# A four-block graph and expert network on one core: X ahead of weights, results ahead of weights, another start of the relational pipeline, and its later roots on ScalarE and VectorE

## The chip, the core and the metric

One core of one Trainium2 chip runs the whole program as one launch. The time is that of the device, in microseconds (us), for one execution. The kernel before was run three times: 1425.54, 1429.92 and 1430.27 us, median 1429.92. One further execution was profiled.

## What is computed

The input is 128 graphs of 64 nodes with 128 features each (8192 rows) and an adjacency matrix of 64 x 64 integers (0 or 1 in these inputs) for each graph. Four blocks follow one another, each with a residual:

```
x = x + gated_graph(layernorm(x), adj)      # 3 layers of a GRU cell on A^T (h W_l), A = (adj != 0)
x = x + experts_1(layernorm(x))             # top 2 of 8, softmax of the two scores, 128 -> 512 relu -> 128
x = x + relational(layernorm(x), adj)       # below
x = x + experts_2(layernorm(x))             # top 2 of 8, each with its layernorm gains, 128 -> 512 gelu -> 128

def _direction(x, W, Wg, b, bg, adj, rel_ids):
    h = x @ W.T
    g = h @ Wg.T
    vals = (h[:, :, None, :] + b) * sigmoid(g[:, :, None, :] + bg)
    onehot = (adj[..., None] == rel_ids).astype(h.dtype)
    return einsum('bnmr,bmrd->bnd', onehot, vals)
relational = relu(_direction(.., "fwd", adj, 2..40) + _direction(.., "bwd", adj^T, 2..40) + _direction(.., "loop", adj^T, [1]))

def _layernorm(x, axis=-1, eps=1e-05):
    m = jnp.mean(x, axis=axis, keepdims=True)
    v = jnp.var(x, axis=axis, keepdims=True)
    return (x - m) / jnp.sqrt(v + eps)
```

Relations 2 to 40 do not occur in these inputs. Their code stands behind a branch on a flag (`general`), on every engine, and is not entered.

## The kernel before, in words

**Tiles and stages.** X stays in SBUF as 64 tiles of 128 rows (two graphs each); 4 tiles are a group (GT), 16 groups the whole. Products run in float16 as a high and a low part. The stages: `opening` (loads, first norm, weights cut into parts), `gated_graph`, `experts "1"`, `relational`, `experts "2"`, `combine`. `hand_over` is a barrier of four engines between a graph stage and its experts; `phase` ends in a barrier of all. Experts work on rows that POOL scattered to their slots (`send`, L643: one indirect DMA for one tile and one of its two choices), and write to `results` in DRAM. The next stage fetches these (`fetch`, L1677, two DMAs a group) and adds them to X (`mix`, L1667, whose two adds appear as L1673).

**The opening's queues.** ScalarE's queue issues X in four loads, then ADJ (L423, L424); behind them stand ScalarE's own instructions, first the cast of the norm (L386). SP's queue issues 20-odd small loads (L286) and then the expert weights W1 and W2 of 2 MB each (L308, L310).

**The gated graph's queue.** SP stores 16 pieces of the second experts' weights to `kept` as they are cut (`keep`, L867), fetching the next ones between (`bring`, L863), and transposes rows by DMA (`turn_start`, L882; `turn`, L874). Groups are worked in quads; `turn_start(QUAD)` transposes the four tiles of the first group of the second quad, for TensorE's first product of it.

**The relational pipeline.** `relational` is written out as 21 steps s = 0 to 20 (`steps`). Each engine runs its own `step(s)` in a fixed order, and in a step works on several groups:

- VectorE: `mixture(s)` (results added, moments, var_a), `los_a(s-1)`, `los_c(s-4)`, `sums(s-3)` (residual add at L2045, moments, var_c at L2050), `values(s-2)`, `scores(s-4)` (L2109, L2113), `router`, `shifts_a(s)` (L2022, c_shift_a), `shifts_c(s-3)`, `v_los(s-2)`.
- ScalarE: `turned_a(s-1)`, `turned_b(s-4)` (c_xT_a, c_xT_b, out of PSUM), `v_his(s-2)`, `norms_a(s)`, `norms_c(s-3)` (each four norms and a cast; the latter's into ROWS), `weigh` (prob, by Sigmoid), `sig(s-1)` (c_sg), `relu(s-2)` (c_rl).
- TensorE: `turn_a(s-1)`, `turn_b(s-4)`, `scores(s-4)`, `values(s-1)`, `neighbours(s-2)`, `rank`.
- POOL: `roots(s)`, one pow (L1793) of both variances to the power −0.5 into c_rs, then SENDS[s] sends.

`router` chooses experts for a batch of two groups (`first_choice`, `second_choice`, L580 to L599) in the step in which the later group has its scores, and in the step after gives them places (`place`, L629 to L637, writes pos). So batches are chosen at s = 5, 7, 9, ... and placed at 6, 8, 10, ...; sends begin at s = 6 with eight a step, four a step from s = 16, 96 in all; the other 32 follow in the experts' stage. After the sixth batch VectorE also makes the table of blocks (`early_table`). SP first reloads the experts' weights from `kept` (2 x 2 MB, L1808), then packs the relations' rows (L1810), then fetches groups 0 and 1, and each later group when a buffer is free.

Of the kernel before, what the change touches and what calls it, by code (L numbers as in the profile page):

```python
# [16 lines left out]
F32 = mybir.dt.float32  # L17
# [225 lines left out]
def opening(nc, block, keep, over, ins, k):  # L243
# [6 lines left out]
    with ExitStack() as ctx:  # L250
# [33 lines left out]
        def _(sp):  # L284
# [22 lines left out]
            small(gbf[:, 1, :], ins["L1_ffn_br"].rearrange("(a e) -> a e", a=1).to_broadcast([P, E]))  # L307
            sp.dma_start(stage[0][:, :].rearrange("p (n d) -> p n d", d=P),  # L308
# [463 lines left out]
def gated_graph(nc, block, keep, over, ins, k, sent):  # L772
# [14 lines left out]
    with ExitStack() as ctx:  # L787
# [70 lines left out]
        def _(sp):  # L858
# [28 lines left out]
            for i in four:  # L887
                bring(i)
            for i in range(N_PIECE):
# [6 lines left out]
            turn_start(QUAD)  # L896
# [786 lines left out]
BATCH = 2  # L1683
ROUTED = 4
EARLY_BATCH = 5


def relational_sends(NG):

    first = ROUTED + BATCH - 1 + 1  # L1690
    n = NG + ROUTED + 1
    wanted = [0 if s < first else 4 * BATCH if s < NG else CARRY for s in range(n)]
# [4 lines left out]
def batch_at(s, late):  # L1697

    n = s - late - ROUTED - BATCH + 1
    return (n // BATCH, late) if n >= 0 and n % BATCH == 0 and n // BATCH < 16 // BATCH else (None, None)  # L1700


def relational(nc, block, keep, over, ins, k, sent):
# [6 lines left out]
    with ExitStack() as ctx:  # L1710
# [38 lines left out]
        gathered = [sem(f"fetched{p}") for p in two]  # L1749
        half, full = sem("half"), sem("full")  # L1750
# [30 lines left out]
        def _(pool):  # L1781
# [4 lines left out]
            def roots(s):  # L1786
                lo, hi = 0 if s < NG else GT, 3 * GT if 3 <= s < NG + 3 else GT
                if s < NG:
                    pool.wait_ge(var_a, s + 1)
                if 3 <= s < NG + 3:  # L1790
                    pool.wait_ge(var_c, s - 2)
                if lo < hi:
                    pool.tensor_tensor(rstd[s % 4][:, lo:hi], var[s % 2][:, lo:hi], k["mhalf"][:, lo:hi], ALU.pow)\  # L1793
                        .then_inc(rooted, 1)

            def step(s):
                roots(s)
                n = sum(SENDS[0:s])
                for i in range(n, n + SENDS[s]):
                    if i % (2 * T) == 0:  # L1800
                        pool.wait_ge(Q.placed, i // (2 * T) + 1)
                    send(pool, k, k["slots"][1], sent, i)
# [415 lines left out]
```

## Time and profile before

| what | us |
|---|---|
| runs, median (range) | 1429.92 (1425.54 to 1430.27) |
| the profiled execution: its own time, its span | 1423.04, 1420.9 |
| opening | 0 to 87.6 |
| gated graph | to about 480 |
| experts 1 | to 800.5 |
| relational | to 1057.4 |
| experts 2, combine | to 1420.9 |
| busy in the span: TensorE, VectorE, ScalarE, POOL | 912.6, 904.0, 763.7, 732.9 |

The span is from the first to the last instruction of the profiled execution; its own time contains a little more. Ends of stages are read from the barriers between them. A busy share of an engine is a mean over stages with different limits, so the list of instructions of a stage, with the idle time before each and what released it, tells more than the table.

### The profile page before, as it was taken

To read this page: it belongs to the slowest core of one execution; us is meant where nothing else is said; L and a number is where in the kernel's file an instruction comes from. 1 tells how busy PE (TensorE), PEld (TensorE's weight loads), DVE (VectorE), ACT (ScalarE), POOL (GpSimd) and SP (SyncE) were. 2 spreads that over 40 slices of the span, in tenths; PEclk is the share of its full clock that TensorE was granted. 3 is DMA by queue.
4 is the path that set the end of the run, shared out by engine and by line. 5 is a ranking of instruction groups with operands and counts; after the bars stand their busy time and mean duration, and the time that the engine had idled before them with its cause. 6 is when DMAs were issued, how large, how long until landed. Compare 5 with 4: busy or idle time off the path is not lost. (4 is left out here: it accounts for less than half of the span.)

```text
span 1420.9 us, 23073 instructions
## 1 busy us (share of the span) xinstructions
PE 912.6 (64%) x5849; PEld 517.1 (36%) x5850; DVE 904.0 (64%) x2437; ACT 763.7 (54%) x1390; POOL 732.9 (52%) x714
## 2 busy tenths in 40 slices
PE   1367778878873267789887066655522877878830
PEld 1244434444432123334576033333311433346620
DVE  5968789999986426556555167776653655544536
ACT  2477757777752135557566056555531765655720
POOL 3511123767757646556555314777666456554550
PEclk9999999999985569999899555555556999988975
DMA  9233221221201514333322421221122353232209
GB/s 266 75 113 95 83 47 28 56 63 46 61 20 39 137 44 107 84 82 70 69 57 53 163 75 61 66 86 49 40 50 65 81 118 75 65 77 59 54 25 349
DMA packets 198299, 115.61 MB, mean 81 GB/s; under 512 B 154988, under 2 KB 175614, under 8 KB 197408
## 3 DMA queue, kind: packets, MB, share of 16 engines
q1 hardware_dynamic: 168144, 69.54, 20.5%
q0 software_dynamic: 17408, 34.13, 7.5%
q10 hardware_dynamic: 12624, 10.49, 2.6%
q8 instruction: 54, 0.88, 0.3%
q14 instruction: 69, 0.57, 0.1%
HBM read 43.80 MB, written 51.61 MB: 67 GB/s over the span
## 5 line engine op out<-in xcount | busy, mean ns | idle before, releaser
L643 POOL DMA_INDIRECT slots<-ROWS,pos x256 | 265.2, 1036 | 90.4 <-issue 71.1
L1510 POOL DMA_INDIRECT results<-e1ys,e1home x144 | 155.8, 1082 | 126.7 <-DVE e1ys L1638 85.8
L1510 POOL DMA_INDIRECT results<-e2ys,e2home x144 | 152.2, 1057 | 131.2 <-DVE e2ys L1638 91.3
L1585 ACT ACTIVATE e1hf<-psum,VT 128x512 f32<-128x512 f32 (+1 forms) x192 | 104.4, 583 | 141.6 <-PE psum L207 82.4
L1604 DVE SCALAR_TENSOR_TENSOR e1hs<-e1hf,e1hs 128x512 f16<-128x512 f32 x144 | 95.9, 691 | 119.4 <-ACT e1hs L1591 77.9
L1585 ACT ACTIVATE e2hf<-psum,VT 128x512 f32<-128x512 f32 (+1 forms) x192 | 104.2, 582 | 123.0 <-remote 69.9
L1604 DVE SCALAR_TENSOR_TENSOR e2hs<-e2hf,e2hs 128x512 f16<-128x512 f32 x144 | 95.1, 689 | 105.5 <-ACT e2hs L1591 81.7
L1362 POOL TENSOR_TENSOR a_Z<-a_Z,a_H 128x512 f32<-128x512 f32 x48 | 68.2, 1422 | 163.2 <-ACT a_Z L1092 160.5
L205 PE MATMUL psum<-e1xT,W 128*128 128x512 f16 (+1 forms) x192 | 67.5, 352 | 43.9 <-issue 22.3
L205 PE MATMUL psum<-a_hT,WHH 128*128 128x512 f16 x144 | 59.4, 412 | 55.6 <-ACT a_Z L1092 47.4
L205 PE MATMUL psum<-e2hs,W 128*128 128x512 f16 (+1 forms) x192 | 64.9, 338 | 42.7 <-DVE e2hs L1604 36.6
L1591 ACT ACTIVATE e2hs<-e2hf 128x512 f16<-128x512 f32 x144 | 86.9, 633 | 0.0
L1591 ACT ACTIVATE e1hs<-e1hf 128x512 f16<-128x512 f32 x144 | 86.9, 631 | 0.0
L205 PE MATMUL psum<-e1hs,W 128*128 128x512 f16 (+1 forms) x192 | 67.0, 349 | 29.5 <-DVE e1hs L1604 21.5
L205 PE MATMUL psum<-e2xT,W 128*128 128x512 f16 (+1 forms) x192 | 66.0, 344 | 28.7 <-ACT e2hf L1585 11.8
L1793 POOL TENSOR_TENSOR c_rs<-c_var,mhalf 128x12 f32<-128x12 f32 (+2 forms) x19 | 38.2, 2012 | 75.1 <-DVE c_var L2050 52.4
L1938 ACT ACTIVATE c_norm_a<-X,c_shift_a,c_rs 128x128 f32<-128x128 f32 x64 | 26.3, 482 | 80.3 <-DVE c_shift_a L2022 72.1
L206 PE MATMUL psum<-e1xT,W 128*128 128x512 f16 (+1 forms) x192 | 67.7, 353 | 2.1 <-issue 2.1
L207 PE MATMUL psum<-e2xT,W 128*128 128x512 f16 (+1 forms) x192 | 65.4, 341 | 5.1 <-issue 5.1
L207 PE MATMUL psum<-e1xT,W 128*128 128x512 f16 (+1 forms) x192 | 67.5, 351 | 1.4 <-issue 1.4
L206 PE MATMUL psum<-e1hs,W 128*128 128x512 f16 (+1 forms) x192 | 66.8, 348 | 2.1 <-issue 2.1
L206 PE MATMUL psum<-e2xT,W 128*128 128x512 f16 (+1 forms) x192 | 65.8, 343 | 2.7 <-issue 2.7
(363 smaller groups left out, 2676.9 us busy)
## 6 DMA issues: line engine op xcount, KB each, us to landing
c_G<-results SPq DMA_DIRECT2D x32, 256.0 KB
d_G<-results SPq DMA_DIRECT2D x32, 256.0 KB, 5.0
slots<-slots SPq DMA_DIRECT2D x16, 264.0 KB
W<-in_L_ffn_W_dram SPq DMA_DIRECT2D x16, 256.0 KB, 3.4
kept<-a_cut SPq DMA_DIRECT2D x16, 256.0 KB, 2.6
slots<-ROWS,pos POOLq DMA_INDIRECT x256
W<-kept SPq DMA_DIRECT2D x2, 2048.0 KB, 10.1
out_dram<-X ACTq DMA_DIRECT2D x16, 256.0 KB, 7.2
```

The source lines that it names most:

```text
L205: pe.matmul(out, lhs(0), rhs(0), start=start, stop=False, skip_group_check=True)
L206: pe.matmul(out, lhs(0), rhs(1), start=False, stop=False, skip_group_check=True)
L207: return pe.matmul(out, lhs(1), rhs(0), start=False, stop=stop, skip_group_check=True)
L643: pool.indirect_dma_start(out=slots, out_offset=bass.IndirectOffsetOnAxis(ap=k["pos"][:, c, t:t + 1], axis=0), in_=k["ROWS32"][:, t, :], i ...
L1362: pool.tensor_tensor(Z[p % 2][:, :], Z[p % 2][:, :], H[p][:, :], ALU.mult).then_inc(zh_sb, 1)
L1510: pool.indirect_dma_start(out=k["results"][m], out_offset=bass.IndirectOffsetOnAxis(ap=home[:, GT * b + q:GT * b + q + 1], axis=0), in_=ys ...
L1585: t = act.activation(hf[c][:, cols], HB[c][:, cols], func, bias=VT[:, bass.ds(e * CH + b1_col + c, 1)], scale=1 / PS)
L1591: act.activation(hs[j][:, 0, c, :], hf[c][:, :], ACT.Copy, scale=AS).then_inc(h_hi, 1)
L1604: dve.scalar_tensor_tensor(out=hs[j][:, 1, c, :], in0=hf[c][:, :], scalar=AS, in1=hs[j][:, 0, c, :], op0=ALU.mult, op1=ALU.subtract).then_ ...
L1793: pool.tensor_tensor(rstd[s % 4][:, lo:hi], var[s % 2][:, lo:hi], k["mhalf"][:, lo:hi], ALU.pow)\
L1938: i = act.activation(out[:, q, :], tile_of(X, GT * g + q), ACT.Identity, bias=shift[:, q:q + 1], scale=scale[:, q:q + 1])
```

## The change

Four edits.

1. In `opening` SP waits for the last load of X (`x_in[LOADS - 1]`) before it issues W1 and W2.
2. In `gated_graph` SP's `turn_start(QUAD)` moves from behind the loop over the 16 pieces to ahead of it.
3. In `relational` SP fetches groups 0 and 1 first, then packs the rows. The weights come back in eight parts of 512 KB, one each behind the fetch of g = 2 to 9.
4. In `relational` the batches are group 0 alone, group 1 alone, and then pairs; they are chosen at s = 4, 5, 7, 9, ... and sends begin at s = 5 with 8, 6 and 2, then eight a step. `place` (`put`) stands between `los_a` and `los_c`. In steps 0 to 5 (`SPLIT`) `shifts_a` and `norms_a` stand early in the step, POOL takes the two roots apart, with up to two sends between, and the choice stands at the step's end. From step 6 on POOL takes no root: ScalarE takes the square root (`deviations`, 13 calls) and VectorE inverts it and makes one step of Newton's on it (`inverses`, four operations, each waiting for the one before).

```diff
@@ opening, SP
+            sp.wait_ge(x_in[LOADS - 1], 16)
             sp.dma_start(stage[0][:, :].rearrange("p (n d) -> p n d", d=P),
...
@@ gated_graph, SP
             for i in four:
                 bring(i)
+            turn_start(QUAD)
             for i in range(N_PIECE):
...
-            turn_start(QUAD)
...
-BATCH = 2
+BATCHES = [(0, 1), (1, 1)] + [(g, 2) for g in range(2, 16, 2)]
 ROUTED = 4
-EARLY_BATCH = 5
+SPLIT = 6
...
-    wanted = [0 if s < first else 4 * BATCH if s < NG else CARRY for s in range(n)]
+    wanted = [0 if s < first else (8, 6, 2)[s - first] if s < first + 3 else 8 if s < NG else CARRY for s in range(n)]
...
@@ relational, POOL
+            def step(s):
+                n, m = sum(SENDS[0:s]), sum(SENDS[0:s + 1])
+                if 3 <= s < SPLIT:
                     pool.wait_ge(var_a, s + 1)
+                    root_of(s, 0, GT)
+                    ahead = min(n + 2, m)
+                    sends(n, ahead)
                     pool.wait_ge(var_c, s - 2)
+                    root_of(s, GT, 3 * GT)
+                    sends(ahead, m)
+                else:
+                    if s < 3:
+                        pool.wait_ge(var_a, s + 1)
+                        root_of(s, 0, GT)
+                    sends(n, m)
...
@@ relational, SP
-            for n, w in enumerate((k["W1"], k["W2"])):
-                sp.dma_start(w[:, :, :].rearrange("p s n -> p (s n)"), k["kept"][n]).then_inc(back, 16)
+            for g in two:
+                fetch(sp, k, 0, g, G[g], gathered[g])
...
+                if 2 <= g < 10:
+                    weights(g - 2)
...
@@ relational, ScalarE
+            def deviations(s):
+                lo, hi = columns_at(s, NG)
+                if s < NG:
+                    act.wait_ge(var_a, s + 1)
+                if s < NG + 3:
+                    act.wait_ge(var_c, s - 2)
+                    act.activation(deviation[s % 2][:, lo:hi], var[s % 2][:, lo:hi], ACT.Sqrt).then_inc(spread, 1)
...
                     turned_a(s - 1, (s - 1) % 2)
+                if s < SPLIT:
+                    norms_a(s, s % 2)
...
                     v_his(s - 2, s % 2)
-                if s < NG:
+                if s >= SPLIT:
+                    deviations(s)
+                if SPLIT <= s < NG:
                     norms_a(s, s % 2)
...
@@ relational, VectorE
+            def inverses(s):
...
+                dve.wait_ge(spread, n + 1)
+                dve.reciprocal(y, deviation[p][:, lo:hi]).then_inc(newton, 1)
+                dve.wait_ge(newton, 4 * n + 1)
+                dve.scalar_tensor_tensor(out=t, in0=y, scalar=-0.5, in1=v, op0=ALU.mult, op1=ALU.mult).then_inc(newton, 1)
+                dve.wait_ge(newton, 4 * n + 2)
+                dve.tensor_tensor(t, t, y, ALU.mult).then_inc(newton, 1)
+                dve.wait_ge(newton, 4 * n + 3)
+                dve.scalar_tensor_tensor(out=rstd[s % 4][:, lo:hi], in0=t, scalar=1.5, in1=y, op0=ALU.add, op1=ALU.mult)\
+                    .then_inc(newton, 1)
+                dve.wait_ge(newton, 4 * n + 4)
...
                     los_a(s - 1, (s - 1) % 2)
+                put(s)
+                if s < SPLIT:
+                    shifts_a(s, s % 2)
...
                     scores(s - 4)
-                router(s)
-                if s < NG:
+                if s >= SPLIT:
+                    choose(s)
+                    inverses(s)
+                if SPLIT <= s < NG:
                     shifts_a(s, s % 2)
...
                     v_los(s - 2, s % 2)
+                if s < SPLIT:
+                    choose(s)
...
```

The order of the built programs at three places follows. Names ahead of the arrow are written, those behind it read. L numbers of the changed program are its own. Semaphores keep the name of the first that had their number, so n_... there is one of the relational stage.

SP at the start of the relational stage, before:

```order
L1808 DMA W<-kept 128x8192 x2
L1810 DMA relrows<-in_L_gnn_b_fwd_dram 39x128
L1810 DMA relrows<-in_L_gnn_bg_fwd_dram 39x128
L1810 DMA relrows<-in_L_gnn_b_bwd_dram 39x128
L1810 DMA relrows<-in_L_gnn_bg_bwd_dram 39x128
L1680 DMA c_G<-results 128x512 x4
L1680 DMA c_G<-results 128x512 [waits c_full,n_x_in2]
L1680 DMA c_G<-results 128x512
```

and now:

```order
L1681 DMA c_G<-results 128x512 x4
L1841 DMA relrows<-in_L_gnn_b_fwd_dram 39x128
L1841 DMA relrows<-in_L_gnn_bg_fwd_dram 39x128
L1841 DMA relrows<-in_L_gnn_b_bwd_dram 39x128
L1841 DMA relrows<-in_L_gnn_bg_bwd_dram 39x128
L1681 DMA c_G<-results 128x512 [waits c_full,n_x_in0]
L1681 DMA c_G<-results 128x512
```

The two loads of W stood ahead of all; now the four DMAs of groups 0 and 1 do.

ScalarE in a step with a choice of experts, before:

```order
L1976 ACTIVATE c_xT_b<-psum 128x1024 [waits n_chain,n_small_sb]
L1959 ACTIVATE c_vs<-c_sg 128x512 [waits n_empty_set,n_w_in1]
L1938 ACTIVATE c_norm_a<-X,c_shift_a,c_rs 128x128 [waits c_shifted_a]
L1938 ACTIVATE c_norm_a<-X,c_shift_a,c_rs 128x128 x3
L1946 ACTIVATE c_tok_a<-c_norm_a 128x512 [waits c_norm_as]
L1938 ACTIVATE c_norm_c<-X,c_shift_c,c_rs 128x128 [waits c_shifted_c]
L1938 ACTIVATE c_norm_c<-X,c_shift_c,c_rs 128x128 x3
L1953 ACTIVATE ROWS<-c_norm_c 128x4x128 [waits c_norm_cs]
L604 ACTIVATE prob<-v_gap 128x8 [waits v_gapped]
L605 ACTIVATE ROWS<-v_gap 128x8
```

and now (the square root first writes c_deviation):

```order
L2015 ACTIVATE c_xT_b<-psum 128x1024 [waits n_consts,n_chain]
L1990 ACTIVATE c_vs<-c_sg 128x512 [waits n_small_done,n_empty_out]
L1998 ACT_TABLE_LOAD [waits c_var_c]
L1998 ACTIVATE c_deviation<-c_var 128x12 [waits c_var_a]
L1969 ACTIVATE c_norm_a<-X,c_shift_a,c_rs 128x128 [waits c_shifted_a]
L1969 ACTIVATE c_norm_a<-X,c_shift_a,c_rs 128x128 x3
L1977 ACTIVATE c_tok_a<-c_norm_a 128x512 [waits c_norm_as]
L1969 ACTIVATE c_norm_c<-X,c_shift_c,c_rs 128x128 [waits c_shifted_c]
L1969 ACTIVATE c_norm_c<-X,c_shift_c,c_rs 128x128 x3
L1984 ACTIVATE ROWS<-c_norm_c 128x4x128 [waits c_norm_cs]
L605 ACT_TABLE_LOAD
L605 ACTIVATE prob<-v_gap 128x8 [waits v_gapped]
```

A load of a table now stands in front of the square root, behind c_vs, and another in front of prob; in a step without a choice the second stands in front of c_sg. There are 13 of each.

VectorE in a step that places a batch, from the scores to c_shift_a, before:

```order
L2109 TENSOR_TENSOR S<-psum,c_rs 128x32 [waits n_chain]
L2113 TENSOR_TENSOR S<-S,gate_b 128x32 [waits n_consts]
L629 TENSOR_TENSOR v_wide<-psum,base 128x64 [waits v_ranked]
L630 TENSOR_TENSOR base<-psum,base 128x8 [waits v_chain]
L631 TENSOR_TENSOR v_wide<-v_wide 128x128 [waits v_chain]
L634 TENSOR_TENSOR ROWS<-prob,ROWS 128x8 [waits v_weighed,v_chain]
L636 TENSOR_REDUCE v_row<-v_wide 128x16
L637 CAST pos<-v_row 128x2x8 [waits v_chain]
L2022 SCALAR_TENSOR_TENSOR c_shift_a<-c_mv,c_rs 128x4 [waits c_rooted]
```

Now the place stands in the first half of such a step, between the two subtractions L240:

```order
L240 SCALAR_TENSOR_TENSOR c_tok_a<-c_norm_a,c_tok_a 128x512 [waits n_w_sb]
L630 TENSOR_TENSOR v_wide<-psum,base 128x64 [waits v_ranked]
L631 TENSOR_TENSOR base<-psum,base 128x8 [waits v_chain]
L632 TENSOR_TENSOR v_wide<-v_wide 128x128 [waits v_chain]
L635 TENSOR_TENSOR ROWS<-prob,ROWS 128x8 [waits v_weighed,v_chain]
L637 TENSOR_REDUCE v_row<-v_wide 128x16
L638 CAST pos<-v_row 128x2x8 [waits v_chain]
L240 SCALAR_TENSOR_TENSOR ROWS<-c_norm_c,ROWS 128x4x128 [waits n_lo]
L2108 TENSOR_TENSOR X<-X,c_rl 128x512 [waits n_small_sb]
```

and from the scores to c_shift_a there are these:

```order
L2172 TENSOR_TENSOR S<-psum,c_rs 128x32 [waits n_consts]
L2176 TENSOR_TENSOR S<-S,gate_b 128x32 [waits n_small_in]
L2071 RECIPROCAL c_guess<-c_deviation 128x12 [waits c_spread]
L2073 SCALAR_TENSOR_TENSOR c_slope<-c_guess,c_var 128x12 [waits c_newton]
L2075 TENSOR_TENSOR c_slope<-c_slope,c_guess 128x12 [waits c_newton]
L2077 SCALAR_TENSOR_TENSOR c_rs<-c_slope,c_guess 128x12 [waits c_newton]
L2084 SCALAR_TENSOR_TENSOR c_shift_a<-c_mv,c_rs 128x4 [waits c_newton]
```

The six operations of the place have left the stretch ahead of c_shift_a, and four of the inverse have come in.

## Rows read from the trace of the kernel before

**Rows 1.** Busy time by stage: window, length, busy us (instructions) by engine, PEclk, DMA share, GB/s.
```profile
0.00:87.60 87.60, 24.72 (x156) 19.24 (x157) 68.14 (x294) 39.03 (x60) 32.51 (x48) 1.00 0.51 138
...
800.50:814.90 14.40, 0.00 (x0) 0.00 (x0) 0.93 (x1) 0.00 (x0) 1.25 (x39) 0.50 0.92 367
...
877.00:1010.00 133.00, 80.98 (x562) 43.89 (x560) 92.62 (x427) 73.62 (x153) 99.59 (x83) 0.50 0.21 67
```

**Rows 2.** Relational stage before the sends, VectorE: start us, us, engine, line, operation, idle before.
```profile
854.05 0.16 DVE L2022 SCALAR_TENSOR_TENSOR c_shift_a<-c_mv,c_rs 128x4 f32<-128x4 f32 x1 [1.47 <-POOL c_rs L1793]
...
859.84 0.69 DVE L2045 TENSOR_TENSOR X<-X,c_rl 128x512 f32<-128x512 f32 x1 [0.35 <-ACT c_rl L1928]
...
866.20 0.15 DVE L2022 SCALAR_TENSOR_TENSOR c_shift_a<-c_mv,c_rs 128x4 f32<-128x4 f32 x1
...
876.89 0.16 DVE L2022 SCALAR_TENSOR_TENSOR c_shift_a<-c_mv,c_rs 128x4 f32<-128x4 f32 x1 [0.19 <-POOL c_rs L1793]
```

**Rows 3.** Relational stage with sends, VectorE.
```profile
940.94 0.69 DVE L2045 TENSOR_TENSOR X<-X,c_rl 128x512 f32<-128x512 f32 x1 [0.21 <-issue]
...
947.06 0.19 DVE L2109 TENSOR_TENSOR S<-psum,c_rs 128x32 f32<-128x32 f32 x1 [3.17 <-remote]
...
950.56 0.15 DVE L2022 SCALAR_TENSOR_TENSOR c_shift_a<-c_mv,c_rs 128x4 f32<-128x4 f32 x1
...
1009.46 0.15 DVE L2022 SCALAR_TENSOR_TENSOR c_shift_a<-c_mv,c_rs 128x4 f32<-128x4 f32 x1
```

**Rows 4.** Waits from 877 to 1010 (us in total, times, longest), and POOL's root there.
```profile
DVE S L2109 <- PE psum L207: 20.0, 6, 4.5
...
DVE c_shift_a L2022 <- POOL c_rs L1793: 0.4, 2, 0.2
...
L1793 POOL TENSOR_TENSOR c_rs<-c_var,mhalf 128x12 f32<-128x12 f32 x9 | 20.7, 2303 | 4.4 <-DVE c_var L2050 4.2
```

**Rows 5.** One step with sends, TensorE and ScalarE.
```profile
944.08 0.17 PE L207 MATMUL psum<-WGATE,c_xT_b 128*128 128x8 f16 x1
...
939.25 0.63 ACT L1953 ACTIVATE ROWS<-c_norm_c 128x512 f16<-128x512 f32 x1
939.78 0.64 ACT L1933 ACTIVATE c_sg<-psum 128x256 f32<-128x256 f32 x2
...
950.75 1.65 ACT L1938 ACTIVATE c_norm_a<-X,c_shift_a,c_rs 128x128 f32<-128x128 f32 x4 [6.20 <-DVE c_shift_a L2022]
```

**Rows 6.** Opening, the same lists, of SP, ScalarE and VectorE.
```profile
11.68 0.90 SPq L308 DMA_DIRECT2D n_stage<-in_L_ffn_W_dram  x1
...
14.63 5.69 ACTq L424 DMA_DIRECT2D ADJ<-in_adj_dram  x1
...
22.31 0.69 DVE L240 SCALAR_TENSOR_TENSOR ROWS<-n_norm,ROWS 128x512 f16<-128x512 f32 x1 [8.46 <-ACT ROWS L386]
```

**Rows 7.** Gated graph, the same lists, of SP and TensorE.
```profile
94.84 1.76 SPq L863 DMA_DIRECT2D W<-in_L_ffn_W_dram  x4
...
102.55 0.60 SPq L867 DMA_DIRECT2D kept<-a_cut  x1
...
179.17 6.47 SPq L882 DMA_TRANSPOSE a_hT<-ROWS  x5
...
185.55 0.58 PE L205 MATMUL psum<-a_hT,WHH 128*128 128x512 f16 x1 [2.91 <-DMA a_hT<-ROWS]
```

**Rows 8.** Hand-over, SP and VectorE, and the page's DMA issue (KB each, us to landing).
```profile
805.29 1.99 SPq L1680 DMA_DIRECT2D c_G<-results  x4
...
814.95 1.42 DVE L1673 TENSOR_TENSOR X<-X,c_G 128x512 f32<-128x512 f32 x2 [13.45 <-DMA c_G<-results]
...
d_G<-results SPq DMA_DIRECT2D x32, 256.0 KB, 5.0
```

**Rows 9.** The table load of the last experts, ScalarE.
```profile
1063.61 1.28 ACT L1585 ACT_TABLE_LOAD   x1 [10.40 <-PE psum L207]
1064.91 1.26 ACT L1585 ACTIVATE e2hf<-psum,VT 128x512 f32<-128x512 f32 x2
```

More of the change, by code:

```diff
@@ L1680, in fetch, with chosen_at, rooted_by, columns_at @@
         sp.dma_start(G[:, c, :, :], rows[:, c, bass.ds(GT * g, GT), :]).then_inc(sem, 16)
-BATCH = 2
+BATCHES = [(0, 1), (1, 1)] + [(g, 2) for g in range(2, 16, 2)]
 ROUTED = 4
-EARLY_BATCH = 5
+SPLIT = 6
 def relational_sends(NG):
-    first = ROUTED + BATCH - 1 + 1
+    first = ROUTED + 1
     n = NG + ROUTED + 1
-    wanted = [0 if s < first else 4 * BATCH if s < NG else CARRY for s in range(n)]
+    wanted = [0 if s < first else (8, 6, 2)[s - first] if s < first + 3 else 8 if s < NG else CARRY for s in range(n)]
     early = 2 * GT * (NG - QUAD)
     return [max(min(w, early - sum(wanted[0:s])), 0) for s, w in enumerate(wanted)]
-def batch_at(s, late):
-    n = s - late - ROUTED - BATCH + 1
-    return (n // BATCH, late) if n >= 0 and n % BATCH == 0 and n // BATCH < 16 // BATCH else (None, None)
+def chosen_at(s):
+    for b, (g, n) in enumerate(BATCHES):
+        if g + n - 1 + ROUTED == s:
+            return b, g, n
+    return None, None, None
+def rooted_by(s):
+    return sum(1 if n < 3 else 2 for n in range(min(s + 1, SPLIT)))
+def columns_at(s, NG):
+    return (0 if s < NG else GT), (3 * GT if s < NG + 3 else GT)
 def relational(nc, block, keep, over, ins, k, sent):
@@ L1784, in _, with root_of, sends @@
             i.then_inc(rv_set, 1)
-            def roots(s):
-                lo, hi = 0 if s < NG else GT, 3 * GT if 3 <= s < NG + 3 else GT
-                if s < NG:
+            def root_of(s, lo, hi):
+                pool.tensor_tensor(rstd[s % 4][:, lo:hi], var[s % 2][:, lo:hi], k["mhalf"][:, lo:hi], ALU.pow)\
+                    .then_inc(rooted, 1)
+            def sends(n, m):
+                for i in range(n, m):
+                    for b, (g, groups) in enumerate(BATCHES):
+                        if i == 2 * GT * g:
+                            pool.wait_ge(Q.placed, b + 1)
+                    send(pool, k, k["slots"][1], sent, i)
+            def step(s):
+                n, m = sum(SENDS[0:s]), sum(SENDS[0:s + 1])
+                if 3 <= s < SPLIT:
                     pool.wait_ge(var_a, s + 1)
-                if 3 <= s < NG + 3:
+                    root_of(s, 0, GT)
+                    ahead = min(n + 2, m)
+                    sends(n, ahead)
                     pool.wait_ge(var_c, s - 2)
[L1792 to L1802, printed above, removed]
+                    root_of(s, GT, 3 * GT)
[5 more added lines that the diff above has]
+                    sends(n, m)
             steps(pool, step)
@@ L1806, in _, with weights @@
         def _(sp):
-            for n, w in enumerate((k["W1"], k["W2"])):
-                sp.dma_start(w[:, :, :].rearrange("p s n -> p (s n)"), k["kept"][n]).then_inc(back, 16)
+            def weights(i):
+                n, part = i // 4, slice(i % 4 * E * HID // 2, (i % 4 + 1) * E * HID // 2)
+                w = (k["W1"], k["W2"])[n]
+                sp.dma_start(w[:, :, :].rearrange("p s n -> p (s n)")[:, part], k["kept"][n][:, part]).then_inc(back, 16)
+            for g in two:
+                fetch(sp, k, 0, g, G[g], gathered[g])
             for n, name in enumerate(("b_fwd", "bg_fwd", "b_bwd", "bg_bwd")):
                 sp.dma_start(relrows[:, n * P:(n + 1) * P], ins["L1_gnn_" + name]).then_inc(rows_packed, 16)
-            for g in two:
-                fetch(sp, k, 0, g, G[g], gathered[g])
             sp.wait_ge(rows_packed, 64)
```

53 lines of the change are left out of this document (32 added, 21 removed).

## The prediction

> **What bounds the kernel now.** I read the table of stages first [rows 1]. The stages follow one another, most of them with a barrier between, so an edit in one is worth what it moves that stage's end, and nothing later hides it. The change touches four: the opening (0 to 87.6 us, VectorE busy 68.1), the gated graph (to 480), the gap from 800.5 to 814.9, in which no engine computes while the DMA share is 0.92, and the relational stage (to 1057.4). No engine fills the last: in 133 us of it POOL is busy 99.6, VectorE 92.6, TensorE 81.0 and ScalarE 73.6. So a chain through the engines bounds it, at a granted clock of 0.50 (1.2 GHz) throughout.
>
> What that chain is the rows of VectorE show, if a step is read as two halves. The first runs from c_shift_a (L2022) to the residual add (L2045): 5.79 us at 854.05, norms, casts and relu on ScalarE back to back. The second runs to the next c_shift_a: 6.36 us with a choice of experts (859.84 to 866.20); the step after, without one, lasts 10.69 in all [rows 2]. There POOL sends nothing, and a pair of steps takes 22.84. Once it sends, a second half with a choice takes 9.62 (940.94 to 950.56), and the nine steps from 876.89 to 1009.46 take 14.73 each, 29.5 a pair [rows 2, 3]: 3.3 us more a step. POOL's root is not the cause, VectorE waits for it 0.4 us in 133 [rows 4]. TensorE's signals arrive late: at 947.06 VectorE starts on scores, 3.17 us idle, whose last matmul began at 944.08 [rows 3, 5]; waits for TensorE in front of the scores sum to 20.0 us in 6 times [rows 4]. Why they are late no row says. This decides the case: the root that the change takes from POOL is not what the chain waits for.
>
> **Opening.** The expert weights (2 x 2 MB) go behind X. ScalarE's queue issues X and then ADJ; ADJ's issue takes 5.69 us, to 20.32, behind it stands the first cast, and VectorE idles 8.46 us for that [rows 6]. From 11.68, when SP issues the weights, to 20.32 two queues share the DMA engines. Alone, ScalarE's would need about half of these 8.6 us: the gain is between 0 and 4.3, I take **−3.3**, nearer the upper end since the wait of 8.46 is larger than all of it. VectorE's 68.1 busy us lie almost all behind that wait, so the gain carries through. The weights come no later in sum: the same bytes, at a DMA share of 0.51 over the stage [rows 1].
>
> **Gated graph.** The four transposes of quad 1 move on SP ahead of the 16 pieces. Five such issues take 6.47 us, four 5.2; SP is free from 96.60 to the first store of a piece at 102.55 [rows 7]. They fit, and the pieces stay where they are. TensorE's 2.91 us at 185.55 for a_hT go [rows 7]: 0 to −2.9. I take **−2.9**; what is late next there would be ScalarE's own chain.
>
> **Hand-over.** SP issues 4 MB of weights and four row loads, then at 805.29 the results, and VectorE starts at 814.95 [rows 8]. The same fetch in the last stage lands after 5.0 us (median) [rows 8]. Issued at 800.5, it starts VectorE at about 806: **−8.9**, the bounds −9.6 (every us of the wait but 4.8) and −4 (only the issues' 4.8 saved, less 0.8). The weights come back in eight parts at steps 2 to 9 beside a DMA share of 0.21 [rows 1], and are needed by the experts alone: nothing.
>
> **Steps 4 to 6.** Groups 0 and 1 are now chosen one by one: one choice and one place more. The choice, 13 chained operations, is 3.05 of the 3.50 us from 947.06 to 950.56 [rows 3], 0.23 us each; the place, six of that kind, 1.4; for four tiles instead of eight both a little less, 4.1 together. Step 6's own loads and Newton are 2.2 (below): 6.3 us. The sends start one step earlier, and with them TensorE's late signals: up to 3.3 more. Between +6.3 and +9.6 I take **+7**, near the lower end, because step 7 now sends only two. Most of the head start is spent here.
>
> **Steps 7 to 15.** From step 6 ScalarE's table is switched twice a step, to Sqrt's and back to Sigmoid's: 13 x 2 = 26 loads by 1.28 us [rows 9]. The first waits for c_var_c and runs where ScalarE waits for c_shift_a anyway, 6.20 us at 950.75 [rows 5]: free where TensorE's signal is late. The second stands between the cast into ROWS and c_sg (or prob), and behind it c_rl, on which L2045 waits. ScalarE has no gap there, 939.25 + 0.63 overlaps 939.78 [rows 5]: **+1.28** a step. On VectorE reciprocal and Newton are four chained operations by 0.23, put between the scores (or the choice) and c_shift_a: **+0.9** a step, in place of a root that cost 0. The place, 1.4 in every second step, moves to where VectorE waits for ScalarE: −0.7 a step at best. A step grows by 1.5 (place hidden whole) to 2.5 (nothing hidden, and the first load in series after c_var_c against one pow of 2.30 [rows 4]). I take 1.9, a little under the middle since the late signals do cover the first load: 9 x 1.9 = **+17**. POOL's 20.7 us of pow in 133 [rows 4] are saved on an engine that this chain does not wait for.
>
> The Trainium skill ("ScalarE: Activation LUTs", section on table sets as the hidden batching unit) wants calls of one set kept together and switches few; this change makes 26. The same page adds a drain of about 1.38 us to each switch. The trace disagrees at the one switch that I show: the Gelu starts 0.02 us after its load ends [rows 9]. By the page this term would be larger by an estimated 26 x 1.38 = 36 us.
>
> **Tail.** Steps 16 to 18 keep loads and Newton but have no norms_a that waits for them. Between 0 and 3 x 2.5 = 7.5; I take **+3**. The last place opens the experts, whose own stages do not change.
>
> **Sum.** −3.3 −2.9 −8.9 +7 +17 +3 = +11.9. The profiled execution took 1423.04 us (span 1420.9), so one like it 1434.9. The median of the runs shown, 1429.92, lies 6.9 above: **1442** as a median, slower by 0.8%.
>
> **Rivals.**
> A: TensorE's late signals come from POOL being nearly full. For it: they are late only where POOL sends. Against it: it still sends as much, and only the 20.7 of its 99.6 busy us go [rows 1, 4]. If two thirds of the 3.3 us a step go in ten steps, that is −22 on my sum: **1420**. It is ahead of no change from 12 us on, 1.2 a step. Faster, 0.17.
> B: the lateness is a time that passes anyway, and part of the added work runs inside it; the 3.17 us at 947.06 are room [rows 3]. ScalarE's rows without a gap behind c_shift_a are against [rows 5]. Then a step grows by 0.6 to 1.2, and the sum is 0 to +6: 1430 to 1436. Within 0.5%, 0.25.
> C: a switch between two calls that lie close together costs ScalarE more than the load, because it must first run empty; taken as the load's own length once more, 26 x 1.28 = +33 on mine: 1475. Against it is the start right behind the load [rows 9], though that one followed an idle of 10.40 us. Slower, 0.04. The Trainium skill's drain ("ScalarE: Activation LUTs", what a table load costs) would be this rival.
> D: the gap does not close, because the results' own short packets fill the DMA engines, not the weights. For it: the share is still 0.92 up to 814.9; against it the 5.0 us of the last stage [rows 1, 8]. +5 on mine, the other end of that term: 1447. Slower, 0.06.
>
> **How the numbers follow.** Half a per cent, 7.1 us, is about what a measurement of this kernel can tell from no change: 1422.8 and 1437.1. Faster 0.17 (A); same 0.25 (B); slower 0.58 (C, D and my own case with 0.48). My own case alone, by the bounds of its terms: 1438 to 1455. To leave out no more than 2 in 10, the range takes in B and half of A: **1419 to 1457**; C and the better half of A stay out.
>
> **What would show it.** 26 more table loads of 1.28 us, the next operation right behind each. VectorE's first add of results near 806. ADJ's issue over by about 17. No wait for a_hT. From c_shift_a to L2045 7.0 us instead of 5.8, steps of 16 to 17 us instead of 14.7, TensorE's signals still late, POOL idle longer. Wrong if steps last 14.7 or less (A; B if up to 15.9), if what follows a load starts over 1 us after its end (C), or if VectorE still starts at 811 or later (D). If the second halves shrink by more than the place's 1.4, A is at work.

## The result, and the profile after

The changed kernel took 1479.47 us as a median of 4 runs (1474.44 to 1485.31), the kernel before 1430.1 (4 runs, 1425.54 to 1451.79). The ratio is 1.0364, 95% interval 1.0298 to 1.043: slower by 49 us, where 12 were forecast. The time lies above the range, which ended at 1457. The profiled execution has a span of 1483.5 us against 1420.9. Here and below a median is of all runs, while a ratio leaves out runs more than 1.5% above the fastest of their kernel, so the two can differ by some tenths of a per cent (after_3 and paced_2 below were profiled in such a longer run).

Where the 62.6 us of the spans are, read from the first and last instructions of each stage:

| stretch | before | after | forecast for it |
|---|---|---|---|
| to the start of the gated graph | 88.1 | 86.1 | −3.3 |
| gated graph, to the first product of experts 1 | 392.2 | 391.8 | −2.9 |
| experts 1, to VectorE's first instruction of the relational stage | 320.3 | 328.0 | 0 |
| from there to the first add of results | 14.4 | 4.4 | −8.9 |
| from there to the first product of experts 2 | 247.1 | 302.8 | +27 |
| experts 2 and the last fetch | 358.9 | 370.4 | 0 |

The expert stages' code is the same. Over the profiled executions on chips where the kernel before takes over 1400 us, experts 1 lasts 317 to 348 us whatever the kernel, so the 19 us that the two expert rows grow tell nothing. What tells is the fifth line: +55.7.

First the small edits. ScalarE's, VectorE's and SP's rows of the opening, after, which answer to [rows 6]:

```profile
14.57 3.88 ACTq L425 DMA_DIRECT2D ADJ<-in_adj_dram  x1
...
20.43 0.69 DVE L240 SCALAR_TENSOR_TENSOR ROWS<-n_norm,ROWS 128x512 f16<-128x512 f32 x1 [6.98 <-ACT ROWS L387]
...
22.42 0.90 SPq L309 DMA_DIRECT2D n_stage<-in_L_ffn_W_dram  x1
```

ADJ's issue takes 3.88 us instead of 5.69 and ends at 18.45, not 17. VectorE's first subtraction moves from 22.31 to 20.43: −1.9. (SP's issue of the weights has moved from 11.68 to 22.42.) At the hand-over (SP, then VectorE, as in [rows 8]):

```profile
805.81 2.04 SPq L1681 DMA_DIRECT2D c_G<-results  x4
...
810.28 1.42 DVE L1674 TENSOR_TENSOR X<-X,c_G 128x512 f32<-128x512 f32 x2 [3.49 <-DMA c_G<-results]
```

SP issues the results within 0.1 us of the barrier and VectorE adds them 4.4 us after it: −10.0, a little more than the −8.9 forecast.

Now the relational stage, the table of stages (window, length, busy us by engine, PEclk, DMA share, GB/s; compare [rows 1]):

```profile
0.00:85.70 85.70, 23.71 (x156) 18.42 (x158) 68.12 (x294) 39.03 (x60) 32.51 (x48) 0.72 0.53 141
...
875.00:1047.50 172.50, 84.68 (x585) 44.71 (x584) 101.41 (x479) 102.97 (x183) 70.67 (x72) 0.50 0.20 61
```

The numbers behind the length are TensorE's products, its weight loads, VectorE, ScalarE and POOL. VectorE is busy 101.4 of 172.5 us and POOL 70.7, both a smaller share than before; the granted clock is 0.50, as it was, so the clock does not explain the growth. (In the opening it reads 0.72 where it was 1.00, but VectorE, busy 68.12 us as before, carries that stage, and it ends 1.9 us earlier.) So the engines stand still somewhere. VectorE's rows of two steps (compare [rows 3]):

```profile
894.88 0.16 DVE L2084 SCALAR_TENSOR_TENSOR c_shift_a<-c_mv,c_rs 128x4 f32<-128x4 f32 x1
...
902.57 0.69 DVE L2108 TENSOR_TENSOR X<-X,c_rl 128x512 f32<-128x512 f32 x1
...
908.61 0.16 DVE L2084 SCALAR_TENSOR_TENSOR c_shift_a<-c_mv,c_rs 128x4 f32<-128x4 f32 x1
...
925.89 0.69 DVE L2108 TENSOR_TENSOR X<-X,c_rl 128x512 f32<-128x512 f32 x1 [11.68 <-ACT c_rl L1959]
...
933.12 0.16 DVE L2084 SCALAR_TENSOR_TENSOR c_shift_a<-c_mv,c_rs 128x4 f32<-128x4 f32 x1
```

From one c_shift_a to the next is a step. The one from 908.61, at whose end experts are chosen, takes 24.5 us, the one from 894.88, in which places are given, 13.7: 38.2 a pair, against 29.5 before and 33 forecast. The first half of the long one, 5.8 us before and 7.0 forecast, is 17.3, of which VectorE waits 11.68 for c_rl. POOL in the same time, and the two waits summed over 875 to 1047.5:

```profile
902.17 1.15 POOL L644 DMA_INDIRECT slots<-ROWS,pos  x1 [17.66 <-DVE pos L638]
...
921.66 0.96 POOL L644 DMA_INDIRECT slots<-ROWS,pos  x1 [0.30 <-issue]
940.41 1.15 POOL L644 DMA_INDIRECT slots<-ROWS,pos  x1 [17.79 <-DVE pos L638]
```

```profile
POOL slots L644 <- DVE pos L638: 73.9, 5, 17.8
...
DVE X L2108 <- ACT c_rl L1959: 48.4, 5, 11.7
```

POOL sends sixteen times in one run, 902.17 to 922.6, then waits 17.79 us for the next positions. Before, a root stood between each eight:

```profile
946.63 2.30 POOL L1793 TENSOR_TENSOR c_rs<-c_var,mhalf 128x12 f32<-128x12 f32 x1
949.13 1.03 POOL L643 DMA_INDIRECT slots<-ROWS,pos  x1 [0.20 <-issue]
```

That root starts right behind the eighth send, which ends at 946.61, and the late signal of [rows 3, 5] is there at 947.06. ScalarE and TensorE in the changed kernel's run of sixteen:

```profile
906.20 1.28 ACT L1998 ACT_TABLE_LOAD   x1
907.49 0.21 ACT L1998 ACTIVATE c_deviation<-c_var 128x12 f32<-128x12 f32 x1
...
913.33 1.28 ACT L1964 ACT_TABLE_LOAD   x1
914.62 0.38 ACT L1964 ACTIVATE c_sg<-psum 128x256 f32<-128x256 f32 x1
922.35 0.38 ACT L1964 ACTIVATE c_sg<-psum 128x256 f32<-128x256 f32 x1 [7.34 <-DMA n_stage<-in_L_ffn_W_dram]
925.26 0.60 ACT L1959 ACTIVATE c_rl<-psum 128x512 f32<-128x512 f32 x1 [2.53 <-remote]
```

```profile
910.11 0.42 PE L207 MATMUL psum<-WREL,c_xT_a 128*128 128x256 f16 x1
...
911.17 0.21 PE L1895 MATMUL psum<-WGATE,ident 128*128 128x8 f16 x1
...
927.75 0.19 PE L205 MATMUL psum<-WGATE,c_xT_b 128*128 128x8 f16 x1 [12.19 <-ACT c_xT_b L2015]
```

TensorE's last product of the values is at 910.11, and the small product that closes the neighbours at 911.17. In the code c_sg waits for TensorE alone (the DMA that its row names as releaser belongs to the opening), and c_rl for TensorE and an earlier add of VectorE's; "remote" names no releaser. ScalarE, which waits for both products in turn, gets the first at 922.35, as the last send ends (922.6), and the second at 925.26, 2.6 us behind it. TensorE itself then stands 12.19 us, since c_xT_b could not be made. This is the kind of late signal that stood there before (3.17 us of idle, [rows 3, 5]), grown with the length of POOL's run.

Not every signal is late. The scores' last product is at 905.01, 2.8 us into the run, and VectorE starts on them at 905.74. The values' first half, with its last product at 907.53, is used at 914.62, inside the run. Between VectorE and ScalarE nothing is late at all: c_shift_a starts at 908.61, and the first norm behind it at 908.80. Nor do all late ones wait for the very end: over the four long steps of this trace the values' last product is used 8.6 to 14.4 us after its start, between 3.9 us before the run's end and 1.8 after it, the neighbours' 14.0 to 14.2 us after theirs, 2.6 behind the run's end. "Held for the run" below is short for this.

And nothing drains at a table load: 906.20 + 1.28 is followed by the square root at 907.49, 913.33 + 1.28 by c_sg at 914.62. The further 1.38 us that the Trainium skill states ("ScalarE: Activation LUTs", what a table load costs) is at none of these loads.

### The profile page after: what moved, and what is told of

It reads as the page before. It is cut to its first block and busy times, and to the rows that moved or that the text cites. A ratio compares the mean times of both kernels' runs of the same rounds, so it can differ in the third digit from the quotient of the medians.

```text
span 1483.5 us, 23181 instructions
## 1 busy us (share of the span) xinstructions
PE 924.2 (62%) x5850; PEld 518.3 (35%) x5851; DVE 916.2 (62%) x2508; ACT 803.0 (54%) x1431; POOL 701.3 (47%) x704
## 5 line engine op out<-in xcount | busy, mean ns | idle before, releaser
L644 POOL DMA_INDIRECT slots<-ROWS,pos x256 | 260.3, 1017 | 201.7 <-DVE pos L638 92.1
L205 PE MATMUL psum<-e2hs,W 128*128 128x512 f16 (+1 forms) x192 | 66.7, 347 | 59.8 <-DVE e2hs L1605 53.3
L205 PE MATMUL psum<-e1hs,W 128*128 128x512 f16 (+1 forms) x192 | 66.7, 347 | 29.4 <-DVE e1hs L1605 19.4
L207 PE MATMUL psum<-e1hs,W 128*128 128x512 f16 (+1 forms) x192 | 66.1, 344 | 3.7 <-issue 3.7
L206 PE MATMUL psum<-e1hs,W 128*128 128x512 f16 (+1 forms) x192 | 66.5, 346 | 2.6 <-issue 2.6
L207 PE MATMUL psum<-e2hs,W 128*128 128x512 f16 (+1 forms) x192 | 66.4, 346 | 1.2 <-issue 1.1
```

Source lines behind the costliest of these rows:

```text
L205: pe.matmul(out, lhs(0), rhs(0), start=start, stop=False, skip_group_check=True)
L206: pe.matmul(out, lhs(0), rhs(1), start=False, stop=False, skip_group_check=True)
L207: return pe.matmul(out, lhs(1), rhs(0), start=False, stop=stop, skip_group_check=True)
L644: pool.indirect_dma_start(out=slots, out_offset=bass.IndirectOffsetOnAxis(ap=k["pos"][:, c, t:t + 1], axis=0), in_=k["ROWS32"][:, t, :], i ...
```

## The experiments

Two theories. **Theory 1**: taking the roots from POOL took away what tied POOL to the steps; its sends go out in runs of sixteen, and TensorE's signals are held for such a run. **Theory 2**: the 26 table loads and their surroundings on ScalarE cost it.

The runs fell on chips of two kinds, and this became part of the finding. On one kind the kernel before takes 1404 to 1452 us (called H below, since signals are held there), on the other 1235 to 1245 (called N). Kernels that were measured together ran on one chip, and all ratios are against before on the same chip. The first expectations of paced, no_load, pool_roots and queues were written when only H was known, so that their times in us are times of H; those four ran on N. "Stage" is the time from the first add of results to the first product of experts 2 in the profiled execution.

| kernel | kind | median | ratio (95%) | stage |
|---|---|---|---|---|
| before | H | 1430.1 | 1 | 247.1 |
| the change | H | 1479.5 | 1.036 (1.030 to 1.043) | 302.8 |
| after_again, the same | H | 1466.7 | 1.036 (1.026 to 1.047) | 300.5 |
| after_3, the same | H | 1487.4 | 1.041 (1.025 to 1.057) | 302.0 |
| after_4, the same | N | 1246.3 | 1.006 (1.004 to 1.008) | 253.1 |
| paced_2 | H | 1435.1 | 1.007 (1.001 to 1.013) | 261.2 |
| paced | N | 1244.4 | 1.005 (1.003 to 1.006) | 253.2 |
| pauses | H | 1418.7 | 1.002 (0.997 to 1.007) | 254.0 |
| no_load_3 | H | 1475.8 | 1.035 (1.023 to 1.048) | 292.2 |
| no_load, no_load_2 | N | 1222.4, 1224.1 | 0.987, 0.988 | 230.9, 231.3 |
| pool_roots_3 | H | 1436.9 | 1.007 (0.992 to 1.022) | 249.1 |
| pool_roots, pool_roots_2 | N | 1227.6, 1227.4 | 0.992, 0.991 | 235.8, 236.2 |
| queues_3 | H | 1427.9 | 0.992 (0.972 to 1.012) | 246.6 |
| queues, queues_2 | N | 1221.7, 1222.2 | 0.986, 0.986 | 230.0, 230.0 |
| queues_split | N | 1243.5 | 1.004 (1.002 to 1.005) | 252.2 |
| queues_pause | N | 1232.8 | 0.995 (0.992 to 0.997) | 240.4 |
| no_sends | H | 1541.2 | 1.087 (1.075 to 1.098) | (374.9) |

**The change itself, again.** `after_again` and `after_3` fell on H, `after_4` on N.

> The changed kernel itself, beside the kernel before on the same chip. In the runs of the first comparison TensorE's signals were held while POOL sent (23 and 28 late signals); in the four runs that followed, on another chip (before: 1238 us), none was late. Theory 1 (the loss is held signals times bursts): where the chip holds no signal the change is worth about 1.0047 like the paced form, 1.000 to 1.008; where it holds them, 1.03 or more. Theory 2 (the loss is in the loads): 1.03 or more on either.

> The changed kernel itself beside before, on whichever chip. Theory 1 (runs of 16 sends times held signals): 1.03 to 1.04 where before takes over 1400 us, 1.003 to 1.008 where it takes 1238. Theory 2 (26 table loads alone): the same loss in us on both, 40 to 50.

> The changed kernel itself beside before. Where before takes 1238 us no signal is held and theory 1 expects 1.003 to 1.008, since POOL's runs of 16 sends then hold nothing up; where it takes over 1400, 1.03 to 1.04 again. Theory 2: 40 to 50 us more on both.

Measured: 1.036 and 1.041 on H, 1.006 on N. The traces of the two kinds show the same step with the same run of sends. On N (after_4), VectorE's half with POOL's run, first and last send:

```profile
812.62 0.16 DVE L2084 SCALAR_TENSOR_TENSOR c_shift_a<-c_mv,c_rs 128x4 f32<-128x4 f32 x1
...
819.82 0.69 DVE L2108 TENSOR_TENSOR X<-X,c_rl 128x512 f32<-128x512 f32 x1 [1.60 <-ACT c_rl L1959]
```

```profile
806.18 1.15 POOL L644 DMA_INDIRECT slots<-ROWS,pos  x1 [17.66 <-DVE pos L638]
...
825.68 0.95 POOL L644 DMA_INDIRECT slots<-ROWS,pos  x1 [0.30 <-issue]
```

From c_shift_a to the add 7.2 us, where H has 17.3, though POOL sends sixteen times from 806.18 to 826.6 here too. The half is the 7.0 of the prediction. Theory 2, which wants 40 to 50 us on both, gets 7.8 on N, and falls as the account of H's loss. The granted clock is not the difference either; it is 0.50 in this stage on both, here N (after_4), window, length, busy us, clock:

```profile
715.00:968.00 253.00, 141.09 (x985) 76.14 (x985) 180.12 (x845) 169.24 (x313) 110.92 (x109) 0.50 0.25 76
```

The two kinds differ in such waits in the expert stages as well, where POOL writes the results by indirect DMAs, in rows of one window (540 to 680 us; waits, us in total, times, longest), first H (before), then N (after_4):

```profile
DVE e1hs L1604 <- ACT e1hs L1591: 33.1, 23, 5.2
...
ACT e1hf L1585 <- PE psum L207: 32.4, 19, 5.2
```

```profile
DVE e1hs L1605 <- ACT e1hs L1592: 24.2, 49, 0.6
...
ACT e1hf L1586 <- PE psum L207: 8.4, 16, 0.6
```

In this window no such wait on N is longer than 0.6 us; on H they reach 5.2. Experts 1 takes 215 us on N instead of 296 to its last product.

**POOL tied to the steps, without a root.** `paced`:

```
+                    if SPLIT <= s < NG:
+                        pool.wait_ge(var_a, s + 1)
+                    if SPLIT <= s < NG + 3:
+                        pool.wait_ge(var_c, s - 2)
                     sends(n, m)
```

> The changed kernel (1479.5 us), but from step 6 on POOL waits for var_a and var_c of the step before it sends, as its roots made it do; no root is taken there. Theory 1 (bursts: without the roots nothing ties POOL to the steps, 16 sends run in one go and TensorE's signals are held until they end): the waits of 11.7 us at the residual add are gone, steps fall from 19.1 us to 16 or 17, the time to 1436 to 1450. Theory 2 (the cost is the 26 table loads and what ScalarE does around them): nothing changes, 1475 to 1485.

> The paced form (POOL waits for var_a and var_c of the step, takes no root) once more beside the change itself. Theory 1: on a chip that holds signals 1436 to 1450 against 1479 for the change; on one that doesn't, equal to the change within 0.3%. Theory 2: equal to the change on both.

Two waits and no other edit take the change from 1.036 to 1.007 on H; the long steps fall from 24.3 to 15.4 us, the short ones rise from 13.7 to 14.4, so 14.9 on average where 16 to 17 were expected. On N they are 14.5 and 13.6, so runs of eight still cost H 0.8 to 0.9 us a step. POOL's rows there:

```profile
908.78 0.96 POOL L644 DMA_INDIRECT slots<-ROWS,pos  x1 [12.71 <-DVE c_var L2117]
...
917.91 0.96 POOL L644 DMA_INDIRECT slots<-ROWS,pos  x1 [0.30 <-issue]
922.03 0.96 POOL L644 DMA_INDIRECT slots<-ROWS,pos  x1 [3.16 <-DVE c_var L2117]
...
938.51 0.95 POOL L644 DMA_INDIRECT slots<-ROWS,pos  x1 [6.47 <-DVE c_var L2117]
```

Eight sends, a wait for c_var of 3.16, eight sends, a wait of 6.47. On N nothing changes (1.005 against 1.006), as nothing is held there.

**Pauses in the run.** `pauses`, after each fourth send:

```
+                    if i % 4 == 3:
+                        pool.tensor_tensor(k["idle"][:, :], k["halves"][:, :], k["mhalf"][:, :], ALU.pow).then_inc(idled, 1)
+                        pool.wait_ge(idled, i // 4 + 1)
```

> The changed kernel with a pow of 2.3 us on POOL, waited for, after every fourth send: bursts of 5 us instead of 20. Theory 1: on a chip that holds signals they come through in the pauses, the waits of 11.7 us shrink to under 5, and the ratio falls from 1.036 to 1.01; on one that doesn't, a little slower than the change (POOL 12.9 + 2.3 us a step are still under its 14.1), 0 to +6 us. Theory 2: no gain on either.

```profile
905.46 0.96 POOL L646 DMA_INDIRECT slots<-ROWS,pos  x1 [0.30 <-issue]
906.44 2.30 POOL L1815 TENSOR_TENSOR idle<-halves,mhalf 128x12 f32<-128x12 f32 x1
909.03 1.15 POOL L646 DMA_INDIRECT slots<-ROWS,pos  x1 [0.29 <-POOL idle L1815]
```

```profile
L2113 DVE TENSOR_TENSOR X<-X,c_rl x13: 683/692/727, 872.0 to 1041.8; 128x512 f32<-128x512 f32 x13
...
  issue: 6.6, 4
  ACT c_rl L1964: 3.4, 2
```

This is the most direct test: POOL is given more work, 24 pows of 2.30 us, and the kernel gets 48 us faster (1.036 to 1.002, which is not told from before). Waits of 48.4 us in front of the residual add shrink to 10.0, and steps are 13.7 and 14.4, within 0.1 of those with no sends at all. So with a gap of 2.6 us after every fourth send no signal is late by much.

**No early sends.** `no_sends`: `relational_sends` returns zeros, and all 128 sends are left to the experts' stage.

> The changed kernel with all 128 sends left to the experts' stage, none in the relational stage. Theory 1: no late signal in that stage on any chip, steps of 13.6 and 14.5 us; the experts start some 100 us later against it, so the whole is 60 to 100 us slower. Theory 2: steps stay at 13.7 and 24.5 on a chip that holds signals.

Steps of 13.6 and 14.4 us on H, against 13.7 and 24.4 with sends. The whole is 74 us slower than the change beside it, within the 60 to 100 expected, since experts 2 begin only after the sends; its "stage" contains them.

**No table loads.** `no_load`: the square root is left out.

```
-                    act.activation(deviation[s % 2][:, lo:hi], var[s % 2][:, lo:hi], ACT.Sqrt).then_inc(spread, 1)
+                    act.activation(deviation[s % 2][:, lo:hi], var[s % 2][:, lo:hi], ACT.Copy).then_inc(spread, 1)
```

> The changed kernel with Copy in place of Sqrt, so that the square root is left out and no table is switched: 26 loads of 1.28 us less. Theory 1 (bursts): the second c_sg is late by the burst in every placing step anyway and hides the load before it; only the choosing steps gain 1.3 each and the waits of 11.7 us stay or grow: 1465 to 1478. Theory 2 (table loads): 1430 to 1445, the waits at the residual add are gone.

> The changed kernel with Copy for Sqrt (the square root is left out, no table is switched), again. Theory 1: on a chip that holds signals the runs of 16 sends stay and so do the waits of about 11 us in every second step: ratio 1.015 to 1.03, far above the 0.987 of the other chip. Theory 2: 0.987 on both.

> The changed kernel with Copy for Sqrt: square root left out, no table switched. Where signals are held, theory 1: 1.01 to 1.03, waits of 10 us at the residual add in every second step. Theory 2: 0.985 to 0.995. Where they are not: 0.988 again, and the difference to the change itself is the price of 26 loads, some 20 us.

On H 1.035 stays of 1.041, a little over the 1.01 to 1.03 that theory 1 named and far from theory 2's 0.995 at most: with no load at all most of the loss is there. The stage is 10 us shorter (292.2), its steps are 11.4 and 25.1. Waits of no_load_3, 870 to 1040:

```profile
POOL slots L644 <- DVE pos L638: 65.5, 5, 16.6
...
DVE X L2108 <- ACT c_rl L1959: 21.5, 3, 13.2
```

On N the same edit is worth 1246.3 − 1222.4 = 24 us (on two chips of this kind, ratios 1.0058 and 0.9871; the stage says 22): 0.9 us for each of 26 loads of 1.28. For no_load theory 1 had named 1465 to 1478 before it was known that there are two kinds; on N that was a miss, on H it held.

**Roots back on POOL.** `pool_roots`: `deviations` and `inverses` are not called; POOL waits for var_a and var_c and takes one pow a step ahead of its sends.

> The changed kernel with the later roots back on POOL as one pow a step, no square root on ScalarE, no Newton on VectorE; queue edits, batches and order as in the change. Theory 1: POOL is tied to the steps again and no loads: steps of 14 to 15 us, 1412 to 1430. Theory 2: the same range, since the loads are gone too. If it stays above 1450, both are wrong and the new batches or the place's position carry the cost.

> The changed kernel with one pow a step on POOL in place of square root and Newton, again. Theory 1: POOL is tied to the steps by its root, so where signals are held it stands near the kernel before: 0.99 to 1.01, the rest of the change (batches, order) costing some 6 us and the queue edits gaining 10 to 13. Theory 2: the same.

> The changed kernel with one pow a step on POOL instead of square root and Newton. Where signals are held, theory 1: runs of eight sends as before, steps of 14 to 15 us, 0.99 to 1.01; theory 2: the same. Where not: 0.991 again.

On H 1.007 (not told from 1), on N 0.991. With the queue edits the only other difference to before is the new batches and order: on N 1227.5 − 1221.9 = 5.6 us slower than the queue edits alone, as 5.8 in the stage.

**Queue edits alone.** `queues`: the kernel before with the diff's three edits on SP.

> The kernel before with the queue edits alone (weights behind X, transposes ahead of the pieces, results fetched first and weights in eight parts): both theories say a gain; by the changed trace 1.9 us at the end of the opening, 0.5 more by the experts, and 8.6 at the first add of results (4.5 us after the barrier instead of 14.4): 1430.1 less 10 to 13, so 1417 to 1421.

> The kernel before with the queue edits alone, again, to have it where the chip holds TensorE's signals (before: 1404 to 1452 us there, 1238 on the other). Theory 1 and 2 alike: 10 to 13 us less than before on either chip.

> The queue edits alone. Where signals are held, both theories: 10 to 13 us less than before, 0.99 to 0.995. Where not: 0.986 again.

On N −16.8 us, more than the 10 to 13 expected, and why it is more was not looked into; on H −12 between medians, with an interval that includes none. On N it is the fastest of the kernels that leave nothing out, and beats before and the change; on H it is not told from before.

**Can shorter runs help the kernel before?** `queues_split` (a root of 4 columns, four sends, a root of 8, four sends) and `queues_pause` (a pow of 128x4 after the fourth of eight).

> The queue edits, and POOL's root in two parts (4 columns 1.14 us, 8 columns 1.67 us), each followed by four of a step's eight sends: runs of sends of 5 us with a root between, no table loads, order and batches as before. Theory 1 (held signals need a run of over some 8 us of sends): on a chip that holds signals steps fall from 14.7 to about 13.5, ratio 0.975 to 0.985; on the other equal to the queue edits alone within 5 us. Theory 2 (only the loads matter): equal to the queue edits on both.

> The queue edits, and in each step's eight sends, after the fourth, a pow of 128x4 on POOL (1.14 us), waited for: runs of four sends instead of eight. Theory 1: where signals are held the steps of 14.7 fall to about 14 (POOL's 10.2 + 2.3 + 1.4), 5 us less than the queue edits alone, ratio 0.985 to 0.99; where they are not, the step is POOL's and grows from 13.5 to 14: ratio 0.989 to 0.993 against 0.986. Theory 2: equal to the queue edits alone on both.

Both ran on N alone, where nothing is held, so the gain on H was not measured. The cost on N is shown. queues_split takes 252 us for the stage, 22 more where at most 5 were expected: the root of the 8 columns stands behind four sends, and VectorE waits for it, 33.5 us in 8 times of 780 to 900:

```profile
DVE c_back_c L2039 <- POOL c_rs L1788: 33.5, 8, 6.8
```

queues_pause costs 11 us, with steps of 14.3 us on average instead of 13.2, 1.1 more for a pow of 1.14: without held signals POOL bounds the kernel before (8 x 1.27 + 2.30 = 12.5 and what lies between), and each us put on it lengthens the step. Its 0.995 is a little over the 0.989 to 0.993 expected.

## Why the prediction was wrong

**The step that failed** is the one on steps 7 to 15: "POOL's 20.7 us of pow in 133 [rows 4] are saved on an engine that this chain does not wait for", together with the 3.3 us a step of late signals, carried over as a constant. That made +17 for nine steps; on H they grew by 34.5. The saved pow, with its wait for c_var_c, was also what kept POOL in step: it split the sends into runs of eight. Without it they run sixteen together, and the lateness is no constant but grows with the run: VectorE waits 3.17 us for the scores at 947.06 before, and 11.68 for c_rl now. The rows to see it stood there: TensorE's signals were late only where POOL sent, and the diff showed POOL from step 6 on with no wait left but the one for pos. "POOL idle longer" was even named as a sign, but not followed to what POOL does before it idles. Rival A had the right cause (POOL's sends) with the wrong sign, since it asked how busy POOL is and not how its work is bunched. The Trainium skill's rule of few switches ("ScalarE: Activation LUTs", section on table sets as the hidden batching unit) is borne out on N, by the 24 us of no_load, but does not name the cause on H: no_load_3 keeps most of the loss without a switch.

**The rest of the sum, term by term.** Between starts of c_shift_a in the traces, in us more than without the change (on H against before, on N against the queue edits alone, as before was not profiled there):

| stretch | forecast | H | N |
|---|---|---|---|
| first c_shift_a to the seventh | +7 | +8.3 | +7.4 |
| nine steps, to the sixteenth | +17 | +34.5 | +7.8 |
| from there to the first product of experts 2 | +3 | +13.0 | +7.8 |

The tail failed too: one more wait for c_rl of 10.10 us stands in it on H (1079.44), and even on N it grows by more than twice the forecast. On N the stage is 253.1 us against 230.0: +23 for the forecast's +27, but that is luck in part, since the nine steps were put too high and the tail too low. By kernels the 23 split into +5.8 for batches and order (pool_roots against queues) and +17.3 for loads, square root and Newton in place of pow. There the loads cost 22.2 and Newton for pow gives 4.9 back, because there POOL's work does bound the step: in queues VectorE waits for its root, here from 780 to 905 (us in total, times, longest), 1.7 us a step, where it waited 0.4 us in 133 on H [rows 4]:

```profile
DVE c_shift_a L2029 <- POOL c_rs L1794: 15.5, 9, 3.1
```

The steps on N take 14.1 us on average, 0.9 more than the 13.2 of the queue edits; the forecast had set 1.9 on top of 14.7. Those 13.2 are 1.8 over the 11.4 of a step without sends, though VectorE waits for no scores there: on N, 1.8 of the 3.3 us that the prediction gave to late signals are there without them.

On H the late signals add the rest. They cost the change 302.8 − 254.0 (pauses) = 49 us and before 246.6 − 230.0 (queues_3, queues) = 17, and 23 + 49 − 17 = 55 is the growth of 55.7.

The bounds of the forecast's terms, added up straight, give 1433 to 1466 and not the 1438 to 1455 that it states for its own case; 1479 lies outside both.

**Opening**: −1.9 instead of −3.3. The half of 8.6 us was too much: with the weights out of the way ADJ's issue still takes 3.88 us of its 5.69, so that sharing had cost it 1.8.

**Gated graph**: 0.4 instead of 2.9. The wait for a_hT is gone: the product that stood at 185.55 starts at 183.89 with no wait. But TensorE, 2.2 us ahead of before at 123.6, is 1.4 behind it at 172.2. The granted clock of that stretch is lower, here before and then after:

```profile
125.00:172.00 47.00, 35.88 (x227) 19.14 (x228) 36.62 (x53) 33.74 (x55) 8.90 (x7) 0.93 0.31 94
```

```profile
125.00:172.00 47.00, 37.03 (x216) 19.03 (x213) 34.18 (x51) 30.69 (x50) 6.54 (x5) 0.82 0.29 90
```

In queues_3, with the same edits and a clock of 0.91 there, TensorE's lead goes from 2.1 to 0.1 us over the same products. So part of it goes at nearly the old clock as well; what takes it was not tested.

**Hand-over**: −10.0 for −8.9, right. **Rival C** (1475) comes near the measured time by chance: no load drains, and without loads most of the loss stays. **Rival B** named 0.6 to 1.2 us a step, and N has 0.9, but not for its reason: on N no late signal of TensorE's is there to hide anything, the first half lasts 7.2 us, the added load in full, and it was POOL's own work that had filled the step. **D** did not happen.

**What stays open.** Why the two kinds of chip differ, and what holds TensorE's signals, no run shows; nor why some late ones come before the run's end. That shorter runs speed up the kernel before on H was not measured.

## What to carry to other kernels

Work that is taken from an engine may be what paces it: before moving it, ask for what that engine would no longer wait, and how the rest of its work would then bunch. Spread bursts of indirect DMAs over the steps, by a wait on the step's own semaphore: two waits took the change from 1.036 to 1.007 on H and cost nothing on N (1.006 and 1.005). And measure on more than one chip: the same change cost 0.6% on one kind and 3.6% on the other.

## What was not expected of the hardware

- On one kind of chip TensorE's semaphore signals come late while POOL issues indirect DMAs in a row: in a run of sixteen (20.4 us) one of 2.8 us into it passed at once, those of 7.9 and 9.0 us came at its end or 2.6 us behind it (910.11 to 922.35, 911.17 to 925.26). With a gap of 2.6 us after every fourth, the waits in front of the residual add fell from 48.4 to 10.0 us. On the other kind, with the same run, the longest wait for c_rl in these steps is 1.8 us, and the kernel before takes 1238 instead of 1430 us.
- A switch of ScalarE's table, between calls that follow at once, takes its 1.28 us and nothing more (the next call starts 0.01 us behind it); for the kernel on N it cost 0.9.
- Adding 24 pows of 2.30 us to POOL made the changed kernel 48 us faster.
